# The sums over the labels of the first layer, counts first and the weighted labels written over the labels

## The reference, cut to what matters

```python
A = adj_f if d == 0 else jnp.swapaxes(adj_f, 1, 2)
A = A[:, :, :NONGT, :]          # 20 neighbours, 11 labels, integers 0 or 1
cond = A.sum(-1)                # the counts
vb = A @ w_bias + b_bias        # the weighted labels, summed
...
mask = cond_adj[:, :, None, :] > 0
aff = jnp.where(mask, aff, NEG) + label_bias[:, :, None, :]
w = jax.nn.softmax(aff, axis=-1)
```

## Time and profile before

| what | value |
|---|---|
| median of 3 runs | 540.01 us (539.89 to 540.03) |
| the profiled execution's own time | 541.79 us |
| its span, first to last instruction | 540.0 us |
| PE busy | 489.0 us, 91% of the span |
| PEld busy | 426.6 us, 79% |
| DVE busy | 341.9 us, 63% |
| ACT busy | 250.3 us, 46% |
| POOL busy | 186.6 us, 35% |
| mean granted clock of PE | 0.965 |

### The profile page before, as it was taken

The page is one execution under the profiler, slowest core; times in us unless marked ns, Lnnn a source line. Parts: engine busy times, 40 slices in busy tenths (PEclk is TensorE's granted clock), DMA queues, the critical chain, the costliest instruction groups (busy, mean ns, idle before and its releaser), DMA issues. The chain is left out here.

```text
span 540.0 us, 10140 instructions
## 1 busy us (share of the span) xinstructions
PE 489.0 (91%) x3893; PEld 426.6 (79%) x3893; DVE 341.9 (63%) x612; ACT 250.3 (46%) x489; POOL 186.6 (35%) x170
## 2 busy tenths in 40 slices
PE   7879888888899989998999899989998999798897
PEld 7777777666799679967997699769986896697787
DVE  4865787675866686668757775778575843560211
ACT  2371341265437643763367345734573466227331
POOL 2074334154235423542344224522362151211022
PEclk9966987799999999999999999999999999989999
DMA  8460390009102630245022602180019004500000
GB/s 255 182 221 20 130 214 3 1 23 221 29 1 76 159 57 1 76 135 81 2 76 101 114 1 76 61 157 1 23 40 175 2 4 131 86 1 4 19 1 22
DMA packets 33424, 40.26 MB, mean 75 GB/s; under 512 B 3168, under 2 KB 28256, under 8 KB 33120
## 3 DMA queue, kind: packets, MB, share of 16 engines
q1 hardware_dynamic: 33376, 39.61, 29.5%
HBM read 28.85 MB, written 10.49 MB: 73 GB/s over the span
## 5 line engine op out<-in xcount | busy, mean ns | idle before, releaser
L1495 PE MATMUL ps<-splz,wh 128*128 128x256 f32 x512 | 109.3, 287 | 0.2 <-POOL splz L409 0.2
L1178 DVE TENSOR_REDUCE nm<-ps 128x2 f32<-128x512 f32 x128 | 84.4, 687 | 24.0 <-PE ps L1706 23.6
L1495 PEld LDWEIGHTS ps<-splz,wh 128*128 128x128 f32 x512 | 86.8, 192 | 2.6 <-issue 2.1
L687 ACT ACTIVATE ya<-ps 128x512 f32<-128x512 f32 x128 | 71.8, 596 | 32.1 <-PE ps L1730 30.3
L409 POOL TENSOR_TENSOR hs<-g,hs 128x512 fp32r<-128x512 f32 x32 | 41.2, 1288 | 97.0 <-ACT hs L745 97.0
L1495 PE MATMUL ps<-splz,wl 128*128 128x256 f32 x256 | 67.3, 284 | 0.0
L1706 PE MATMUL ps<-kst,qst 96*128 96x256 f32 x256 | 54.2, 312 | 4.8 <-DVE nm L1178 2.7
L1495 PE MATMUL ps<-wh,hs 128*128 128x256 f32 x256 | 54.3, 284 | 0.0
L1730 PE MATMUL ps<-qst,kst 100*128 100x256 f32 x256 | 49.4, 303 | 3.4 <-ACT ya L687 2.1
L1730 PEld LDWEIGHTS ps<-qst,kst 100*128 100x128 f32 x256 | 37.0, 189 | 15.8 <-ACT ya L687 9.7
L1495 PEld LDWEIGHTS ps<-splz,wl 128*128 128x128 f32 x256 | 49.4, 193 | 0.0
(11 more groups left out here) (139 smaller groups left out, 994.9 us busy)
## 6 DMA issues: line engine op xcount, KB each, us to landing
qk_d<-ya SPq DMA_DIRECT2D x16, 512.0 KB, 3.3
qst<-qk_d SPq DMA_DIRECT2D x24, 256.0 KB, 5.6
kst<-qk_d SPq DMA_DIRECT2D x48, 128.0 KB, 6.3
adjD<-adj SPq DMA_DIRECT2D x8, 440.0 KB, 4.6
ya<-wall SPq DMA_DIRECT2D x12, 256.0 KB, 6.9
xT<-xt SPq DMA_DIRECT2D x8, 256.0 KB, 3.0
x_add<-x SPq DMA_DIRECT2D x8, 256.0 KB, 2.9
result<-xr SPq DMA_DIRECT2D x8, 256.0 KB, 2.2
```

The lines of the kernel that those rows point to most:

```text
L687: act.activation(ex[:, h % EXR], ps[:, h % 2].rearrange("p (c s) -> p c s", c=TC), ACT.Exp, scale=SCALE).then_inc(ex_ok.sem, 1)
L1178: dve.tensor_reduce(nm[:, :, h], ps[:, h % 2].rearrange("p (c s) -> p c s", c=TC), AX.X, ALU.max, negate=True).then_inc(mx_ok.sem, 1)
L1495: ins = pe.matmul(dst, lhs(a, k), rhs(c, k), start=first_ and n == 0, stop=last_ and n == len(todo) - 1, **kw)
```

## The change

`adjm` becomes three steps, called in the same place, one after the other. `adjcount` takes the counts from `adjD` and raises a new semaphore, `cnt_ok`. `adjweigh` waits for it and writes the product of labels and weights over `adjD` itself, read afterwards as floating point. `adjsum` waits for the product and sums it. The wait for `prob_ok` and the tile `prod` are gone. Nothing else is moved.

```diff
-        prod = aff[:].rearrange("p c d h m -> p (c d h m)")[:, 0:2 * TC * M * L].rearrange("p (n l) -> p n l", l=L)
...
-            def adjm(b):
+            counts = cw[:].rearrange("p a d c m -> p a (d c m)")
+            weighted = adjD[:].bitcast(FP32)
+
+            def adjcount(b):
                 dve.wait_ge(adj_in.sem, adj_in.at(b))
                 if b == 0:
                     dve.wait_ge(wb_in.sem, wb_in.at(0))
-                else:
-                    dve.wait_ge(prob_ok.sem, prob_ok.at(b - 1))
-                flat = cw[:].rearrange("p a d c m -> p a (d c m)")
-                dve.tensor_tensor(prod, adjD[:], wb[:, 0:L].unsqueeze(1).broadcast_to([P, 2 * TC * M, L]), ALU.mult).then_inc(prod_ok.sem, 1)
-                dve.tensor_reduce(flat[:, 0, :], adjD[:], AX.X, ALU.add)
+                dve.tensor_reduce(counts[:, 0, :], adjD[:], AX.X, ALU.add).then_inc(cnt_ok.sem, 1)
+
+            def adjweigh(b):
+                dve.wait_ge(cnt_ok.sem, cnt_ok.at(b))
+                dve.tensor_tensor(weighted, adjD[:], wb[:, 0:L].unsqueeze(1).broadcast_to([P, 2 * TC * M, L]), ALU.mult).then_inc(prod_ok.sem, 1)
+
+            def adjsum(b):
                 dve.wait_ge(prod_ok.sem, prod_ok.at(b))
-                dve.tensor_reduce(flat[:, 1, :], prod, AX.X, ALU.add).then_inc(adj_ok.sem, 1)
+                dve.tensor_reduce(counts[:, 1, :], weighted, AX.X, ALU.add).then_inc(adj_ok.sem, 1)
```

More of the change, by code:

```diff
@@ L189, in build @@
         kbt_ok, vblk_ok, kblk_ok, q0T_ok = sig("kbt_ok"), sig("vblk_ok"), sig("kblk_ok"), sig("q0T_ok", 2)
-        prod_ok, adj_ok, off_ok, msk_ok = sig("prod_ok"), sig("adj_ok"), sig("off_ok"), sig("msk_ok")
+        cnt_ok, prod_ok, adj_ok, off_ok, msk_ok = sig("cnt_ok"), sig("prod_ok"), sig("adj_ok"), sig("off_ok"), sig("msk_ok")
         am_ok, aa_ok, amx_ok, asub_ok, aexp_ok, asum_ok, arc_ok, prob_ok = (
@@ L1243, in head @@
                 qcols()
-                adjm(0)
+                adjcount(0)
+                adjweigh(0)
+                adjsum(0)
                 selfadd(0)
@@ L1267, in head @@
                 pTv(1)(0)
-                adjm(1)
+                adjcount(1)
+                adjweigh(1)
+                adjsum(1)
                 yadd(0)
@@ L1305, in head @@
                 mx(3)(0)
-                adjm(2)
+                adjcount(2)
+                adjweigh(2)
+                adjsum(2)
                 yadd(1)
@@ L1350, in round_ @@
                 al(it - 2)
-                adjm(it + 1)
+                adjcount(it + 1)
+                adjweigh(it + 1)
+                adjsum(it + 1)
                 x2add(it - 2)
```

## The result

| what | before | after |
|---|---|---|
| median of the runs that were compared | 540.44 us (6 runs, 539.89 to 541.88) | 544.72 us (6 runs, 543.18 to 545.33) |
| span of the profiled execution | 540.0 us | 543.4 us |
| its own time | 541.79 us | 545.16 us |
| mean granted clock of PE | 0.965 | 0.959 |

The ratio is 1.0059, with a 95% interval from 1.0034 to 1.0085: slower by 3.2 us, where 1.5 us had been predicted. (The two medians are 4.3 us apart; 1.0059 is what comes out against the second three of the six runs of before, 541.38, 541.88 and 540.86 us, while the first three are the 540.01 us that the prediction starts from.) The sign is right, the size isn't, and 544.72 us lies outside the predicted range of 539.9 to 543.1 us.

The account below looks back on a forecast made before the run. The prediction took PE, busy for 91% of the span, as the bound, waiting in each round for DVE's `yadd`. 540.01 + 1.20 + 0.24 + 0.00 + 0.07 gave 541.52, say 541.5 us, range 539.9 to 543.1 us.

Parts of the forecast that it names:

- What bounds the kernel: In each round PE's `rsum` waits 1.31 to 1.32 us for DVE's `yadd`; DVE's row from `al` is on the path.
- The product in place, at nothing: On DVE, the product written over its input costs nothing: 1.06 us, within 0.02 us either way.
- 0.12 us for a wait between neighbours: On DVE, waiting for the instruction right ahead costs 0.12 us; two waits make the three instructions 3.18 us instead of 2.94.
- The rival that the waits are free: DVE drains between any two instructions anyway, so the two waits cost nothing: 540.0 us, chance 0.07.
- 5 x 0.24 us in the rounds: Rounds 2 to 6: `x2add`, `yadd` and PE's `rsum` each start 0.24 us later, 1.20 us in all.
- Element 0, +0.24 us: In the head, `selfadd` has no idle time ahead and every link to PE is tight, so the full 0.24 us.
- Element 1: Product stretched by POOL, last sum 0.44 us later, hidden by `yadd`'s 3.04 us wait for PE: 0.
- element 2's undisturbed product: In the head, the product one place later runs without POOL beside it, at 1.06 us; the element adds 0.07 us.
- The sum, 1.51 us: Whole kernel: 1.20 for the rounds plus 0.24, 0.00 and 0.07 for elements 0, 1 and 2.
- The clock, and the base: PE's granted clock counted as unchanged, 0 us; the base was 540.01 us, from runs agreeing to 0.14 us.
- one fall more: Rival: longer PE idling at `rsum` lowers the clock once more, costing up to 1.6 us: 543.1 us, chance 0.13.
- The size of one fall, up to 1.6 us: PE: high clock instead of low over 3.2 us of dense work saves at most half, 1.6 us.

Follow-up runs that it names:

- e9_delay_clean: Kernel before plus three small 12-element DVE instructions behind the sums, waiting for nothing, their tile allocated behind all others; 543.22 us, ratio 1.0029.
- e4_late_sum: Changed kernel with the weighted sum moved behind `yadd` in the rounds and for element 2, behind `selfadd` for element 0; 539.55 us, ratio 0.9941.
- e7_interleaved: e4_late_sum with the rounds reordered to counts, `x2add`, product, `yadd`, weighted sum, product still written over `adjD`; 538.47 us, ratio 0.9965.
- e11_interleaved_prod: Kernel before, product in its own tile, rounds ordered product, `x2add`, counts, `yadd`, weighted sum; late sum for elements 0 and 2 too; 538.50 us, ratio 0.9947.
- e2_two_waits: Kernel before, order and tile unchanged, with counts waiting for the product and weighted sum for the counts; 543.90 us, ratio 1.0041.
- e12_best: e7_interleaved plus an unused tile of 96 bytes per partition behind `kbt`; 536.85 us, ratio 0.9924.

## Why the prediction was right, and where it wasn't

- **What bounds the kernel.** Right. All of DVE's row from `al` to `yadd` is on the path: e9_delay_clean puts 0.22 us there, and the period grows by 0.24 us. What I missed is a second reader of the same lateness, PE's wait for `xr` (e4_late_sum).
- **The product in place, at nothing.** Right: 1.07 us instead of 1.06 in the rounds, and e7_interleaved and e11_interleaved_prod agree to 0.01 us in the period.
- **0.12 us for a wait between neighbours.** Right: starts 1.09 to 1.11 us apart instead of 0.98, 3.19 us for the three where 3.18 was forecast. The rival that the waits are free is refuted by e2_two_waits, and with it, for these instructions, the sentence of the Trainium skill's page "VectorE: DVE Perf Modes", section "The DRAIN you can't avoid", that a semaphore after each costs the same as one at the end. The page measured that on eight copies. The same section also says that a next instruction that isn't held starts earlier, which the prediction left out; the starts 0.98 us apart at durations of 1.06 us agree with that.
- **5 x 0.24 us in the rounds.** Right in kind, a little small: 0.29 us for each period in this trace, 0.26 to 0.27 in the other three of kernels with two waits. What goes beyond 0.24 is not explained.
- **Element 0, +0.24 us.** Too large: `selfadd(0)` moved by 0.10 us. In the earlier trace rows it started 1.12 us behind the weighted sum's start, where 0.98 is the pace without a wait, so 0.14 us of the 0.24 lay in a pause that was there already, too short for the row to show it as idle time; what it waited for isn't known. I took the missing idle time for a tight link. Element 1 went as worked out (the product 2.09 us, `yadd` hides it with 2.67 us left), and so did element 2's undisturbed product. What element 2 then adds can't be told: `yadd(1)` starts at 90.36 us in before, and at 90.50 and 90.16 in the two traces of the change.
- **The sum, 1.51 us.** At equal clock it is +1.67 us with an error of 0.3, and +1.70 for the waits alone. This part of the prediction holds within the error, with the reserve above that some of the 1.67 us may be the clock's. The parts shift: 1.3 to 1.45 us in the rounds (0.26 to 0.29 each) instead of 1.20, and 0.10 us for element 0 instead of 0.24.
- **The clock, and the base.** This is the step that failed. The sum has the clock at nothing and starts from three runs: I wrote that "the runs agree to 0.14 us, so the falls aren't near a tipping point", and gave one fall more a chance of 0.13. The three lay by chance at the low end of a spread of 8 us: before's median over 117 runs is 541.33 us, 1.3 us above my 540.01, and 85% of them lie above 540.0. The sign of it was in my hands, the profiled execution at 541.79 us, which I carried over as a fixed difference.
- **More time at the low clock.** The falls differ from run to run: the changed kernel spends 43.3 us at the low clock on average, before 38.6 (errors 0.8 and 0.4). At 0.25 us for each us that is 4.7 x 0.25 = 1.2 us. With the 1.67 us it gives 2.85 us, the difference of the mean spans (542.40 against 539.55); the fit is made so that these agree, so that is no proof of its own. The forecast set right by base, clock and delay is 541.5 + 1.3 + 1.2 + 0.16 = 544.2 us, and the 18 runs of the changed kernel have a median of 544.13. That the lateness is what brings more time at the low clock is likely and not shown. All four kernels whose rounds are 0.24 us or more longer have 41.1 to 43.3 us of it and all others at most 40.0; but e9_delay_clean, the delay without the waits, has 41.1 us with an error of 1.1, against 39.2 in the 35 runs of before on its chip.
- **The size of one fall, up to 1.6 us.** Right for the fall at 424 us, 1.4 to 1.5 us in the four traces that have it. Too small for that of before at 472 us, which comes to 2.03 us in the pair of traces.

## What to carry to other kernels

Look for the engine whose row of instructions runs without a pause into another engine's wait: an instruction that waits for the one right ahead of it costs there, and one of another chain placed between them takes the wait away; better still, put what nobody soon needs behind the instruction that is waited for (here 3 us of 540, against 1.5 us lost). Three runs that agree to 0.14 us say nothing about how stable the falls of the clock are: here they stood for a spread of 8 us. Take the base from many runs, read each run's mean clock beside its time, and let the range have room for a share of the clock about as large as the delay itself (here 1.2 us beside 1.67).

## What I hadn't expected of the hardware

- Moving the tiles by 96 bytes per partition, with the same instructions, changed the pace of PE: 0.13 us in a period of 56 us, with 282 instead of 284 ns as the mean of 256 matmuls. The 282 ns are there in e12_best too, but two of its four periods aren't shorter, so what becomes of the gain depends on more than the shift.
- The same program spreads over 8 us in 541, and its time at the low clock goes with it: 0.25 us of span for each microsecond at 1.2 GHz, less than the half that dense work would lose. Some of the falls do lie on stretches in which PE idles (busy for 0.00 of the 0.50 us from 32.00 on the earlier trace rows); that this is the reason is my reading and wasn't tried.
- A fall of the clock near 424 us is in all four traces of the kernels with the two waits, and in none of the ten others. The other falls behind the rounds change from run to run of one kernel: the two traces of the change have 516 us (6.8 us long) and 471.5 us (6.8 us), those of before 472.3 us (3.4 us) and 468.0 us (6.8 us).
